# DVE takes the second scan maximum of a group ahead of the low part of the probabilities

## The reference

```python
x: (4, 256, 64, 64) float32                    # N = 64 * 64 = 4096 pixels
xf = x.reshape(B, C, N)
f = einsum('kc,bcn->bkn', w1, xf) + b1         # 16 rows
energy = einsum('bkn,bkm->bnm', f, f)          # 4096 x 4096 for each image
attention = softmax(energy, axis=-1)
out = einsum('bcm,bnm->bcn', xf, attention)
x = x + 0.1 * out.reshape(x.shape)
y = conv3x3(sign(x), mean(|w|) * sign(w))      # w: (256, 256, 3, 3)
out = batch_norm(y) * gamma + beta + x
```

## Time and profile before

| | us |
|---|---|
| median of 3 runs | 2083.57 (2081.54 to 2087.14) |
| profiled execution | 2082.55 |
| its span, first to last instruction | 2080.8 |
| TensorE matmuls busy | 1940.4 (93%) |
| VectorE busy | 1590.0 (76%) |
| ScalarE busy | 1435.3 (69%) |
| GpSimd busy | 1196.1 (57%) |
| mean granted TensorE clock, whole span | 0.963 of full speed |

### The profile page before, as it was taken

One profiled execution on the slowest core, in us unless ns is written; L12 is line 12 of the kernel. 1 busy time (PEld: TensorE's weight loads), 2 busy tenths in 40 slices (PEclk: granted clock), 3 DMA queues, 4 the chain that ended last, 5 costly groups with the idle time before them and its releaser, 6 DMA issues. The chain is left out here.

```text
span 2080.8 us, 40199 instructions
## 1 busy us (share of the span) xinstructions
PE 1940.4 (93%) x15232; PEld 1636.3 (79%) x15232; DVE 1590.0 (76%) x2167; ACT 1435.3 (69%) x2829; POOL 1196.1 (57%) x791
## 2 busy tenths in 40 slices
PE   4499999999999999999999999999999999989990
PEld 1179998999789888997899999987899997854440
DVE  2477777888887888888787788888887787647778
ACT  2467777777777777777777777777777778643326
POOL 0265555666765555567755556667666664167760
PEclk6589999999999999999999999999999999999995
DMA  3311111012211111012111110021111003224019
GB/s 101 103 38 49 58 59 38 30 30 69 91 47 57 58 38 38 31 60 71 49 53 54 58 38 30 31 81 61 31 30 31 30 29 119 107 98 165 0 40 363
DMA packets 58278, 133.55 MB, mean 64 GB/s; under 512 B 9328, under 2 KB 9328, under 8 KB 57584
## 3 DMA queue, kind: packets, MB, share of 16 engines
q1 hardware_dynamic: 58096, 131.10, 18.7%
HBM read 84.48 MB, written 33.62 MB: 57 GB/s over the span
## 5 line engine op out<-in xcount | busy, mean ns | idle before, releaser
L670 POOL CAST Ph<-P 128x1024 fp32r<-128x1024 f32 x480 | 689.6, 1438 | 585.5 <-ACT P L461 585.0
L471 ACT ACTIVATE sc<-sc,nb 128x512 f32<-128x512 f32 x1024 | 676.2, 660 | 412.8 <-DVE nb L546 412.4
L546 DVE TENSOR_REDUCE nb<-sc 128x1 f32<-128x512 f32 x1024 | 695.2, 684 | 318.0 <-PE sc L381 317.7
L389 PE MATMUL acct<-Ph,xh 64*128 64x512 f32 x2048 | 811.8, 396 | 0.0
L389 PE MATMUL accb<-Ph,xh 64*128 64x512 f32 x2048 | 809.1, 395 | 1.5 <-ACT tb L481 1.3
L389 PE MATMUL accb<-Ph,xl 64*128 64x512 f32 x2048 | 803.5, 392 | 0.0
L389 PE MATMUL acct<-Ph,xl 64*128 64x512 f32 x2048 | 798.0, 390 | 0.0
L556 DVE TENSOR_TENSOR Pl<-P,Ph 128x1024 fp32r<-128x1024 f32 x512 | 664.2, 1297 | 53.8 <-POOL Ph L670 27.1
L389 PE MATMUL acct<-Pl,xh 64*128 64x512 f32 x2048 | 637.6, 391 | 0.0
L389 PE MATMUL accb<-Pl,xh 64*128 64x512 f32 x2048 | 635.0, 389 | 1.5 <-DVE Pl L556 1.4
L461 ACT ACTIVATE P<-ee 128x1024 f32<-128x1024 f32 x512 | 525.5, 1026 | 61.9 <-PE ee L373 42.8
(11 more groups left out here) (105 smaller groups left out, 1370.1 us busy)
## 6 DMA issues: line engine op xcount, KB each, us to landing
wk<-xt SPq DMA_DIRECT2D x32, 512.0 KB, 4.1
xres<-x SPq DMA_DIRECT2D x32, 512.0 KB, 4.3
x<-xres SPq DMA_DIRECT2D x32, 512.0 KB, 2.8
R<-rd SPq DMA_DIRECT2D x32, 256.0 KB, 3.2
xn<-x SPq DMA_DIRECT2D x16, 512.0 KB, 11.9
xr<-x SPq DMA_DIRECT2D x16, 512.0 KB, 11.2
out<-xr SPq DMA_DIRECT2D x16, 512.0 KB, 4.0
An<-x SPq DMA_DIRECT2D x14, 512.0 KB, 5.8
```

The costliest lines, as they stand in the source:

```text
L389: return pe.matmul(to[:], w[rows, g * GM + k, c * 128:(c + 1) * 128], p[rows, s, k * QC:(k + 1) * QC], start=g == 0 and i == 0, stop=g == ...
L471: nc.scalar.activation(sc[v % 2][:], sc[v % 2][:], ACT.Exp, bias=nb[:, t % 2, w:w + 1], accum_out=bsum[:, t % 2, w:w + 1]).then_inc(bsum_d ...
L546: nc.vector.tensor_reduce(nb[:, t % 2, w:w + 1], sc[v % 2][:], AX.X, ALU.max, negate=True).then_inc(nmax_done, 1)
L670: nc.gpsimd.tensor_copy(Ph[:, e % RP, :], P[:, e % 2, :]).then_inc(ph_done, 1)
```

## The change

In each step DVE's two `block_max` now stand next to each other, with `lower` behind them. Where `scale_top(t, 0)`, `row_max` or `row_sum` follow in a step, they follow `lower` directly.

```diff
                 if u < NG:
                     block_max(2 * u)
+                if u < NG:
+                    block_max(2 * u + 1)
                 if 0 <= e - 1 < NG:
                     lower(e - 1)
                 if g == G - 1 and t >= 0:
                     scale_top(t, 0)
-                if u < NG:
-                    block_max(2 * u + 1)
                 if g == 8 and 0 <= t + 1 < NT:
                     row_max(t + 1)
```

## The result

The changed kernel takes 2152.7 us (median; 2152.34 to 2154.2), the old one 2082.56 in the same comparison: a ratio of 1.0334 with a 95% interval of 1.0316 to 1.0352. The forecast was 2162, slower, with a range of 2118 to 2208. The span grew by 70.0 us, from 2080.8 to 2150.8.

The account below looks back on a forecast made before the run. The prediction took TensorE to bound the kernel, busy 51.91 of 52 us in a quiet stretch. Terms 40 + 41 - 5 + 3 = 79 us on 2082.55 gave 2162 us, 3.8% slower, range 2118 to 2208.

Parts of the forecast that it names:

- TensorE has nothing to spare, and the change spends the low part's slack: Quiet step: TensorE waits for nothing, so no gain; the low part's slack falls from 1.9 to 0.3 us.
- The quiet step's loop through the port, 0 us: Low part to low part through POOL takes 3.24 us against TensorE's 3.22; remaining slack absorbs the creep, cost 0.
- a sign of being wrong: Quiet step: the forecast counts as wrong if the step shows 3.3 us or more.
- rival (c): POOL holds the port to its record's end, so the port sets the step at 3.38 us; 2213 us, chance 0.12.
- The end of a block, 40 us: At g = 15 the scaling behind the low part ends late and stalls TensorE: 30 x 1.32 = 40 us.
- The row sum, 41 us: At g = 10 the row sum starts behind the low part and waits for POOL: 29 x 1.42 = 41 us.
- The bound that I worked out without it: Row sum's low end: POOL wins no more races than today, stall 1.33 us, 29 x 0.81 = 23 us.
- The changes of image, -5 us: Around the batch changes the second maximum's wait is cured but the low part stays late: -5 us, bounds -29 to +20.
- Rival (a), faster,: Second maximum no longer waits behind a late low part; needs low part at 1.3 at g = 15; 2039 us, chance 0.06.
- Rival (b): One stall, not two: row sum keeps its 2.11 us and all batch loss comes back; 2120 us, chance 0.15.
- the small places: Projections waiting for the exponential in 12 steps, 2 us, and block 30, 1 us: +3 us.

Follow-up runs that it names:

- e10: Changed kernel with one wait more: POOL's high part starts only when the step's low part is done; 2123.0 us.
- e4: Changed kernel, new order throughout, but at g = 15 DVE scales the top half ahead of the low part; 2121.8 us.
- e1: Changed kernel with the old order in the steps g = 15 alone; 2126.0 us.
- e13: Changed kernel with POOL's first add of x moved from g = 10 to g = 9; 2119.5 us.
- e8: Old kernel with the new order only in the steps around a change of image; 2085.7 us, ratio 1.0016.
- e3: Changed kernel with the old order in the steps g = 10 and g = 15; 2110.9 us, ratio to the old kernel 1.0148.
- e9: Changed kernel with the old order at g = 9, 10, 14 and 15; 2111.1 us.
- e11: e3 with POOL's high part made to wait until the step's low part is done; 2153.5 us.
- e12: Old kernel with POOL's first add of x moved from g = 10 to g = 9; 2075.8 us, ratio 0.9974.

## Why the prediction was right, and where its sizes were off

- **TensorE has nothing to spare, and the change spends the low part's slack.** Right. In a quiet step TensorE now waits for Pl and ScalarE for the low part, waits of which the old step had none, and the step is 3.30 us in the rows shown (3.27 on average, 3.26 before).
- **The quiet step's loop through the port, 0 us.** The mechanism was right; one hand-over was too small. I gave 0.04 us from the low part's end to the exponential; it takes 0.09. So the loop takes 3.30 us instead of 3.24, and the low part's end moves by 0.05 a step instead of 0.02 (3.93, 3.98 and 4.04 at g = 1, 2 and 3 on average). It does not stop at 3.9: at g = 13 it is 4.36, and there the loop sets the step, 3.31 us. Over all quiet steps that is 5 us; their mean of 3.27 stays under the 3.3 that I had named as a sign of being wrong, the step shown reaches it. The port let go 0.14 us before the high part's record ended (0.56 of overlap, 0.42 of waiting), the figure that I took from the earlier trace rows; it was 0.13 or 0.14 in all 405 low parts of the changed kernel that met one POOL instruction already running. So the full hold of rival (c) did not come about, though its step set by the port is there at g = 13 to 15. e10, which takes the meeting away, shortens the step at g = 0 by 0.41 us.
- **The end of a block, 40 us.** Right in mechanism (e4, e1), a little small: 45 us in 26 blocks, 1.73 each instead of 1.32, and the difference is the low part's end at 4.3 instead of 3.9.
- **The row sum, 41 us.** This term was mis-sized: 0.76 us a block instead of 1.42, so 18 us in the 24 blocks away from a change of image, and 28 with the other six. The first of the two waits came as reckoned (1.28 us for the multiply, behind the add of x). The second did not: the subtraction began 0.01 us behind POOL's next high part and took 0.15 us, not the 1.04 that I gave it. The bound that I worked out without it, 0.81 a block or 23 us, was nearer. e13 shows that the port's wait carries this term: without the add of x these steps take 3.30 us, less than the old kernel's 3.44.
- **The changes of image, -5 us.** Right only for the steps there other than g = 0, 11 and 12 (-8); with those three the stretch costs 3. The waits moved as I had said, from ScalarE's maximum to the low part. e8, in its choice of steps, had no gain there by itself.
- **Rival (a), faster,** fell on its own condition: at g = 15 the low part starts at 2.72 on average, not by 1.3, and the scaling behind it is late. **Rival (b)** came near in its first half, the row sum, and not in its second.
- **The sum.** 79 reckoned, 70 measured. Over all blocks the ends cost 47 us instead of 40, the row sum 28 instead of 41 and the quiet steps 5 instead of 0; the rest around the changes of image gave back 8 instead of 5, and the small places 2 where I had put 3 on top. That the sum is so near is partly luck: a term 13 too large met two that were 12 too small together.

What stays open: why e3 keeps 29 us, with the old order at the two places. By place, 28 of them lie at g = 0 to 2 and at g = 11 to 15, behind the two steps in the old order. e9 and e11 show that they move when the switch between the orders moves, and that POOL's time against DVE's has a hand in it; a split by cause was not found.

## What to carry to other kernels

An instruction moved up in one engine's queue pushes what it passes: look up when each piece pushed back is wanted, and what is queued behind it at rare steps (a block's end, a row sum), since that is where most of the loss was here. The maximum that was 0.13 us late in a quiet step was not what TensorE waited for there. Where two engines exclude each other at a port, think of their instructions as one queue in order of arrival: making one shorter can let the wrong one in first, and a wait taken away in one place can come back at an instruction nobody had looked at (the row maximum in e10). Here moving one POOL instruction to another step gained (e12), where the reordering lost.

## What was not expected of the hardware

Halving POOL's rounding, from 1.04 to 0.62 us, made the changed kernel 30 us slower (2152.7 to 2182.7) and the old one 26 us faster (2082.97 to 2057.3). A DVE instruction that already waits for the port gets it ahead of POOL's next one: in the row sum shown, the low part waited at 889.70 for the high part and went before the add of x, which had started at 890.22 and took 2.27 us. A subtraction of 128x4 took 1.25 or 1.26 us in all 26 blocks of the two kernels in which POOL's add of x had started 0.07 us ahead of it, and 0.15 us in all 26 of the changed kernel in which POOL's high part had started 0.01 or 0.02 us ahead; whether the lead or the kind of instruction decides, no run here tells.
